# Layer 0's receiver rows in a four-layer graph-attention kernel: 16 transposes a batch replaced by one transpose, a scratch in memory and two broadcast transfers, with new turn tables

## What is computed

```python
Wh = (h @ W).reshape(B, N, 4, 64)
s_src = einsum('bnhd,hd->bnh', Wh, a_src);  s_dst = einsum('bnhd,hd->bnh', Wh, a_dst)
e = s_src[:, :, None, :] + s_dst[:, None, :, :]
e = where(e > 0, e, 0.2 * e);  e = where(adj != 0, e, -inf)
alpha = softmax(e, axis=2)
h_out = einsum('bijh,bjhd->bihd', alpha, Wh);  return elu(h_out)
```

## Time and profile before

| | |
|---|---|
| median of 3 runs | 2844.16 us (2843.12 to 2851.12) |
| the profiled execution's own time | 2851.32 us |
| its span, first to last instruction | 2849.4 us |
| mean granted TensorE clock | 0.992 |
| busy share of the span: PE, PEld, DVE, ACT, POOL | 98%, 88%, 86%, 80%, 23% |

### The profile page before, as it was taken

How to read it: one execution, slowest core, us unless ns; L and a number is a source line. 1 busy time by engine, 2 the same in 40 slices (tenths; PEclk the granted TensorE clock), 3 DMA queues, 4 the chain that set the end, 5 groups by cost and what they waited for, 6 DMA issues and landing times.

```text
span 2849.4 us, 63430 instructions
## 1 busy us (share of the span) xinstructions
PE 2803.5 (98%) x23704; PEld 2499.1 (88%) x23704; DVE 2455.1 (86%) x6405; ACT 2285.3 (80%) x6079; POOL 642.4 (23%) x1051
## 2 busy tenths in 40 slices
PE   7999999999999999999999999999999999999997
PEld 7888998888988898898898888888998988888885
DVE  6798888988888988888988889988889888889874
ACT  5687878888888888888788788888788888887785
POOL 5021122221122221122212122211122211222111
PEclk9999999999999999999999999999999999999997
DMA  2000000000000000000000000000000000000000
GB/s 82 9 1 16 16 16 16 16 1 16 16 16 16 9 9 16 16 16 16 2 16 16 16 16 16 1 16 16 16 16 16 2 16 16 16 16 9 2 8 15
DMA packets 16785, 41.83 MB, mean 15 GB/s; under 512 B 5344, under 2 KB 7392, under 8 KB 16480
## 3 DMA queue, kind: packets, MB, share of 16 engines
q1 hardware_dynamic: 16480, 37.77, 3.8%
HBM read 20.99 MB, written 16.78 MB: 13 GB/s over the span
## 4 chain that ended last, share of the span: by engine, by line
PE 92%; DVE 5%; ACT 2%; issue 1%; POOL 0%; DMA 0%; POOLq 0%; DVEq 0%; ACTq 0%
PE bank L597 49%; PE bank L695 22%; PE bank L729 9%; PE bank L683 4%; PE bank L647 4%; DVE R L920 1%; PE bank L816 1%; PE bank L671 1%; PE bank L767 1%; PE bank L773 0%; DVE Z L1015 0%; DVE oTlo L1021 0%; PE bank L706 0%; PE bank L707 0%; ACT Z L608 0%
## 5 line engine op out<-in xcount | busy, mean ns | idle before, releaser
L695 PE MATMUL bank<-hw,R 128*128 128x257 f32 x3072 | 727.5, 384 | 1.7 <-ACT hw L1241 1.2
L695 PEld LDWEIGHTS bank<-hw,R 128*128 128x128 f32 x3072 | 564.6, 191 | 92.3 <-issue 11.5
L1422 POOL TENSOR_TENSOR rs<-ve,mhalf 128x4 f32<-128x4 f32 x128 | 140.4, 1097 | 1722.4 <-DVE ve L863 1679.6
L920 DVE SCALAR_TENSOR_TENSOR R<-bank,E,mask_ne 128x512 f32<-128x512 f32 x640 | 451.1, 742 | 5.4 <-PE bank L683 4.2
L597 PE MATMUL bank<-wfc_hi,oThi 128*128 128x256 f32 (+1 forms) x1024 | 299.8, 293 | 0.0
L597 PE MATMUL bank<-wfc_hi,oTlo 128*128 128x256 f32 (+1 forms) x1024 | 288.7, 282 | 0.0
L597 PE MATMUL bank<-wfc_lo,oThi 128*128 128x256 f32 (+1 forms) x1024 | 288.5, 282 | 0.0
L729 PEld LDWEIGHTS bank<-hw,R 128*64 128x64 f32 x8192 | 251.4, 138 | 37.2 <-issue 34.6
L729 PE MATMUL bank<-hw,R 128*64 128x65 f32 x8192 | 269.6, 224 | 2.8 <-DVE R L920 2.8
L1220 ACT ACTIVATE Z<-bank,rs 128x258 f32<-128x258 f32 (+1 forms) x384 | 176.3, 479 | 50.0 <-PE bank L597 48.3
L1438 POOL TENSOR_TENSOR Z<-Z 128x128 f32<-128x128 f32 x256 | 114.9, 479 | 409.9 <-ACT Z L1218 232.9
(11 more groups left out here) (293 smaller groups left out, 8381.4 us busy)
## 6 DMA issues: line engine op xcount, KB each, us to landing
x<-in_x_dram SPq DMA_DIRECT2D x32, 512.0 KB, 3.6
out_dram<-x SPq DMA_DIRECT2D x31, 512.0 KB, 2.6
R<-in_adj_dram SPq DMA_DIRECT2D x2, 512.0 KB, 6.2
Z<-in_L_gnn_mlp_w_dram SPq DMA_DIRECT2D x2, 512.0 KB, 5.6
O<-in_L_gnn_W_fc_dram SPq DMA_DIRECT2D x1, 1024.0 KB, 7.1
out_dram<-x SPq DMA_DIRECT2D x4, 128.0 KB, 1.8
...
```

The source lines that it names most:

```text
L695: ins = e.matmul(bk[:, 0:257], P[:, j, i * 128:(i + 1) * 128], hw[:, j, 0:257], start=(j == 0), stop=(j == NBLK - 1))
L920: e.scalar_tensor_tensor(P[:, t, :], bank_of(b, "row", p)[:, :], m["E"][:, 1, h, j:j + 1], mask[:, j, :], ALU.max, ALU.mult).then_inc(up(" ...
L1422: e.tensor_tensor(m["rs" + z][:, :], m["ve" + z][:, :], mhalf[:, :], ALU.pow).then_inc(up("rs", b), 1 if l == 1 else 3)
```

## The change

For layer 0 of the batches 1 to 31 (`by_dma`), the receivers' rows take another way; batch 0 and the other layers keep the old one. The function `gather` on PE turns all four heads at once: one transpose of the 128x16 piece of E into 16 partitions x 128 columns of a PSUM bank. DVE copies these 16x128 values into a corner of Z (`turned_row`), and that frees the bank. SP writes them to a scratch in memory, `rows_dram` (8 KB), waits for the write to land, and reads them back twice, each time with every one of the 128 partitions reading the same 4 KB: heads 0 and 1 into the tile hT hi, heads 2 and 3 into hT lo (512 KB in SBUF each). Then `weigh` reads its row from hT in SBUF where it read a PSUM bank before. The tables of turns of all engines are other ones, and in SP's table the load of a batch's x stands in its own batch's program. The semaphores of the score vectors' loads are joined to those of the weights, so a wait for weights of groups 2, 4, 5 and 6 counts 48 instead of 16. The tables' strings are left out below.

```diff
+ROW_LAYERS = (0,)
+LATE = 0
...
+def by_dma(b, l):
+
+    return l in ROW_LAYERS and 0 < b < B - LATE
...
+    def row(p, l):
+        return ("rT", l, "sc", (l, 5)) if by_dma(b, l) else ("row", p, "P", (p, 3))
...
-        + [("TM0", 0, "sc", (0, 1)), ("row", 0, "P", (0, 3))]
+        + [("TM0", 0, "sc", (0, 1)), row(0, 0)]
         + [u for h in range(4) for u in (
-            ([("row", h + 1, "P", (h + 1, 3))] if h < 3 else []) + [("att0", h, "y0", (h,))])]
+            ([row(h + 1, 0)] if h < 3 and not by_dma(b, 0) else []) + [("att0", h, "y0", (h,))])]
         + [("hT1", k, "hTlo", (1, k)) for k in range(2)] + [("m1", i, "m1a", (i,)) for i in range(4)]
         + [("h1", i, "hAlo", (i,)) for i in range(4)]
...
+        s_kept = [new_sem(f"kept{s}") for s in range(LANES)]
+        s_rows = [new_sem(f"rows{s}") for s in range(LANES)]
         s_wl = [new_sem(f"wl{n}") for n in range(7)]
-        s_al = [new_sem(f"al{n}") for n in range(7)]
+        s_al = [new_sem("al0"), None, *s_wl[2:]]
+        WL = [16, 16, 48, 16, 48, 48, 48]
         s_adj = [new_sem(f"adj{n}") for n in range(2)]
...
+        row_d = nc.dram_tensor("rows_dram", (LANES, 16, 128), F32, kind="Internal").ap()
+        moves = [[(b, l) for b in range(lane, B, LANES) for l in ROW_LAYERS if by_dma(b, l)] for lane in range(LANES)]
+
+        def staged_row(s, l):
+
+            return ends[s][0:16, 512:640] if l == 0 else f32(hT[s]["hi"][0:4, 0, 0:128])
+
+        def rows_of(s, l, h):
+
+            return f32(hT[s][PARTS2[h // 2]][:, h % 2, :]) if l == 0 else f32(hT[s]["lo"][:, 0, :])
+
+        def at_kept(b, l):
+            before = moves[b % LANES][:moves[b % LANES].index((b, l))]
+            return s_kept[b % LANES], 16 * (len(before) + sum(k == 0 for _, k in before) + 1)
+
+        def at_rows(b, l, h):
+            before = moves[b % LANES][:moves[b % LANES].index((b, l))]
+            if l == 0 and h > 1:
+                sem, value = at_kept(b, l)
+                return sem, value + 16
+            return s_rows[b % LANES], 16 * (len(before) + 1)
...
+            def gather(l, nh):
+                w.wait_ge(*freed(b, "rT", l))
+                w.wait_ge(*at("E", b, l, 0))
+                e.transpose(bank_of(b, "rT", l)[0:NBLK * nh, 0:128], m["E"][:, 0, 0:nh, :].rearrange("p h n -> p (h n)"),
+                            ident[:, :]).then_inc(up("row", b), nh)
+                yield
+
             def row(p, l, h):
+                if by_dma(b, l):
+                    yield from gather(l, 1)
+                    return
                 w.wait_ge(*freed(b, "row", p))
                 bk = bank_of(b, "row", p)
...
             yield from top(0, 4)
-            yield from row(0, 0, 0)
+            if by_dma(b, 0):
+                yield from gather(0, 4)
+            else:
+                yield from row(0, 0, 0)
             for h in range(4):
-                if h < 3:
+                if h < 3 and not by_dma(b, 0):
                     yield from row(h + 1, 0, h + 1)
...
+            def turned_row(l, nh):
+                if by_dma(b, l):
+                    w.wait_ge(*at("row", b, {0: 3, 2: 5, 3: 6, 4: 7}[l]))
+                    if l == 0 and b >= LANES:
+                        w.wait_ge(*at("x3", b - LANES, 3, 1))
+                    e.tensor_copy(staged_row(s, l), bank_of(b, "rT", l)[0:NBLK * nh, 0:128]).then_inc(up("sc", b))
+                    yield
...
                 w.wait_ge(*at("E", b, l, 1))
-                w.wait_ge(*at("row", b, p))
+                if by_dma(b, l):
+                    w.wait_ge(*at_rows(b, l, h))
+                    row = rows_of(s, l, h)
+                else:
+                    w.wait_ge(*at("row", b, p))
+                    row = bank_of(b, "row", p)[:, :]
                 for j in range(NBLK):
                     t = (4 * p + j) % PTILES if p < 4 else j
                     if 4 * p + j >= PTILES and p < 4:
                         w.wait_ge(*at("att0", b, (4 * p + j - PTILES) // 4, (4 * p + j - PTILES) % 4))
-                    e.scalar_tensor_tensor(P[:, t, :], bank_of(b, "row", p)[:, :], m["E"][:, 1, h, j:j + 1],
+                    e.scalar_tensor_tensor(P[:, t, :], row, m["E"][:, 1, h, j:j + 1],
...
         def sync_batch(e, w, b):
-            n = b + LANES
-            if n < B:
-                if n >= XSLOTS:
-                    w.wait_ge(xout[n % XSLOTS], 16 * (n // XSLOTS))
+            s = b % LANES
+            if b >= LANES:
+                if b >= XSLOTS:
+                    w.wait_ge(xout[b % XSLOTS], 16 * (b // XSLOTS))
                 else:
                     w.wait_ge(s_id, 1)
                     w.wait_ge(s_wlo, K_BEFORE[7] - 2)
                     w.wait_ge(s_wA, 8)
-                e.dma_start(xs[n % XSLOTS][:, :, :], x_v[n]).then_inc(xin[n % XSLOTS], 16)
+                e.dma_start(xs[b % XSLOTS][:, :, :], x_v[b]).then_inc(xin[b % XSLOTS], 16)
             yield
+            for l in ROW_LAYERS:
+                if by_dma(b, l):
+                    nh = 4 if l == 0 else 1
+                    w.wait_ge(*at("sc", b, l, 5))
+                    e.dma_start(row_d[s, 0:NBLK * nh, :], staged_row(s, l)).then_inc(s_kept[s], 16)
+                    yield
+                    w.wait_ge(*at_kept(b, l))
+                    every = row_d[s].rearrange("(h n) q -> h (n q)", n=NBLK)
+                    if l == 0:
+                        e.dma_start(f32(hT[s]["hi"][:, :, :]), every[0:2].partition_broadcast(128)).then_inc(s_rows[s], 16)
+                        e.dma_start(f32(hT[s]["lo"][:, :, :]), every[2:4].partition_broadcast(128)).then_inc(s_kept[s], 16)
+                    else:
+                        e.dma_start(rows_of(s, l, 0), every[0].partition_broadcast(128)).then_inc(s_rows[s], 16)
+                    yield
             if b < B - 1:
                 w.wait_ge(*at("x3", b, 3, 1))
                 e.dma_start(o_v[b], xs[b % XSLOTS][:, :, :]).then_inc(xout[b % XSLOTS], 16)
```

276 lines of the change are left out of this document (139 added, 137 removed), and 2 rows, old and new, of the table SHARED.

## The result

The changed kernel takes **2860.8 us** (median of 4 runs, 2859.68 to 2862.77) against 2844.55 for the kernel before on the same chip: a ratio of 1.0052, 95% interval 1.0037 to 1.0067. It is slower by 15 us (11 to 19). The forecast was 2798 us with a range to 2828, so the time lies outside the range and on the other side.

A forecast was written before the change was run, and what follows sets the result against it. PE, busy 99.9% of the middle, was taken as the bound: -51 us on PE, +4 for small holes, +1 for batches 1 and 2, so -46 from a median of 2844.2 to 2798 us; 8-in-10 range 2780 to 2828.

The forecast's parts named there:

- PE's saving: On PE, 496 row transposes removed save 55 us, one added transpose a batch costs 3.7: net 51 us less, bounds 36 and 70.
- The way: Rows from gather to hT by copy, write and reads: 6.6 us for heads 0 and 1, at most 10.1, hidden in the middle.
- Rival three: Broadcast read at a quarter of a load's rate takes 14.4 us, beyond the cover; slower, about 2875 us; chance 0.04.
- +4 for small holes: PE in the middle: its 3.4 us of idle time about doubles, adding 4 us to the sum.
- PE busy 99.9%: Kernel before, the 2500 us middle: PE has no holes, so work removed from PE leaves the time if no hole replaces it.
- the rows' cover: Other lanes' work between gather or copy and first use: 13.8 and 16.5 us on PE, 13.2 on DVE, longer than 10.1.
- I take no change from 742: DVE's weighs: reading the row from SBUF instead of a bank leaves each at 742 ns.
- rival four: DVE and POOL contend as weighs read two SBUF operands: 11 us of DVE, far end 77 and about 2875 us; chance 0.02.
- Against it: DVE would still be at 93%: Argument against DVE and POOL contention costing time: even at its far end DVE would be only 93% busy.
- what would show it: Trace signs: PE above 99.6% busy, period 86.7 us, 528 transposes, weighs near 742 ns, reads 3 to 8 us, few DMA waits.
- signs of being wrong: PE waiting for layer 0's weighed tiles; reads over 12 us; third, DVE's longer queue leaving PE holes over 1 us a batch.
- rival one: Rows late in part, PE standing 0.3 to 1 us a batch more: 2808 to 2835 us; chance 0.14.

The follow-up runs named there:

- e1: Changed kernel's turns with the old way of the rows: 16 transposes a batch back on PE, weighs read a bank, no row transfers; 2932.1 us, 1.0309.
- e9: The rows' new way in the turns of the kernel before, the copy right ahead of the batch's first weigh on DVE; 3056.2 us, 1.0745.
- e2: Changed kernel with the two broadcast reads a batch replaced by two 8 KB writes, weighs reading stale rows; 2860.8 us, 1.006.
- e3: Changed kernel with POOL's centring and partial sums cut to 4 columns from batch 3 on; 2826.5 us, 0.994.
- e4: Kernel before with POOL's centring and partial sums cut to 4 columns from batch 3 on; 2842.9 us, 0.9991.
- e17: Kernel before, turns and transposes kept, with 496 layer 0 weighs reading their row from hT in SBUF instead of the bank; 2855.1 us, 1.0025.
- e5: Changed kernel with layer 0's weighs on 384 of 512 columns from batch 3 on; 2833.9 us, 0.9961.

## Why the prediction was wrong

**PE's saving was right.** Forecast -51 us; the records of the row kinds, the gather included, take 52.6 us less by steps (116.0 against 59.4 + 4.0), and e1 against after gives 49.7. Transposes fell from 1024 to 528.

**The way was right, with its cover.** Reads landed after 3.9 and 4.8 us against 3.6 to 7.1; the copy took 272 ns against 284; DVE had no wait for a transfer. Without cover the kernel lost 8.5 us a batch (e9), not 6.6. DVE's own wait was 4.2 of it, and the granted clock was lower too (0.962 against 0.996). Rival three had nothing: e2.

**The term that failed is "+4 for small holes".** PE's waits grew by 40.8 us, and the prices of its other products by 18.1. With -49.7 that is +9.2, the difference of PE's own spans. Against my -46 this is 55 us; the other 7 is that the profiled execution of before lay 7 us above its median, and that of after did not. Of these 59 us lost, 25.6 go with POOL's work: the waits fall by 32.3 from after to e3 and by 6.7 from before to e4. Some 9.6 are the 17 new pairs of denominators and transposes, which the table has among the prices and which are waits for DVE as well. The remaining 24 are small waits that DVE and ACT make in the new order, and what is left of the prices; no run takes them apart. I read "PE busy 99.9%" as slack of the others that the change would leave alone. But the turns are part of the change. A new table is a new kernel, and its cover for every other wait had to be looked at as I looked at the rows' cover. The order showed the pairs back to back before any run.

**The second step that failed is "I take no change from 742".** It rested on L1030 and L1044: 684 ns with one operand in a bank, 682 with both in SBUF. That compared operations wherever they happened to stand. The same row that I used for rival four had the sign: 705 for the form that reads rowt. With POOL light in the kernel before (e4) the two forms take 685 and 684. The right reading is by what POOL does meanwhile. The weighs grew by 16.7 us beside the 8.4 of the copies.

**Rival four had the mechanism and the wrong price and chance.** I put it at 11 us of DVE from the 23 ns, 77 at the far end, and gave 0.02. By e3 it is worth about 30 us of time. Its cost on DVE lay between the bounds; what I missed is that the new turns pass such delays on where the old ones mostly don't, at the same busy share of DVE (88.6% in the changed kernel, 88.7% in e17). In the old turns 22 us more of DVE's busy time (e17) cost 7 us, in the new ones 47 us less (e3) gave 32 and 56 less (e5) gave 27. "Against it: DVE would still be at 93%" was no argument, as the share of busy time says nothing of whether each result is early enough for an order fixed beforehand.

The Trainium skill (SBUF — State Buffer, the section "Who interferes with whom") says that a DVE instruction with two SBUF inputs contends with a GpSimd one that reads SBUF, and one with a single SBUF input, outside the 2-port modes, doesn't. This case's trace agrees on who: 744 against 917 to 934 ns from hT, 739 to 749 from a bank. The same page of the Trainium skill calls this an exclusive lock, by which the one that comes second stands. This trace doesn't contradict it. At 1489 us the second subtraction began when 0.59 us of the first weigh's record were left and took 0.45 us more than the 0.455 of one beside a bank's weigh; the second weigh began when 0.40 us of that subtraction were left and took 0.20 more than 744 ns. They grew by 0.14 and 0.19 us less than what was left of the other's record. How much of a record is the reading itself, the trace doesn't show.

**Of "what would show it"**, three signs held (528 transposes; reads in 3 to 8 us; no DVE wait for transfers) and three didn't: the middle's PE busy share 98.9% and not 99.6, the period 88.71 and not 86.7, the weighs from hT lo 775 to 820. Of the signs of being wrong the third all but came: PE's idle time in the middle grew by 0.84 us a batch. The sums are right, but rival one's 1 us a batch ends at 2829, not at 2835. The range was too narrow because each rival was priced alone, on the old order's slack.

**Open:** without POOL's work on either side, the changed kernel's waits are still 15.2 us above the kernel before (e3 against e4). That the new order makes them and the 18 us of prices is the reading of e1, whose own waits (62 us) partly come from the old rows standing where they weren't meant to. Whether an order exists in which the change gains wasn't found.

No version that computes every output with the new rows beats the kernel before. With the sums in fp32 the changed kernel is equal to the kernel before with the same sums, and 0.2% behind the kernel before itself.
